# Row maxima over whole rows of 4096 columns in two chunks, with the first conversions and maxima of those chunks placed around the first steps

## The reference, cut to what matters

```python
scores = (Wh @ a1)[:, None] + (We @ a2)[None, :]
e = jnp.where(scores > 0, scores, ALPHA * scores)      # 0.2 in layer 0, 0.01 in layer 1
e = jnp.where(adj > 0, e, NEG_BIG)
attention = jax.nn.softmax(e, axis=1)
h_prime = attention @ entity_embs                      # layer 0; attention @ wh in layer 1
x = _layernorm(x + elu(h_prime + x))                   # layer 0; layer 1: x + out + bias
```

## Time and profile before

| | us |
|---|---|
| median of three runs | 627.31 |
| lowest and highest | 624.94, 627.68 |
| the profiled execution | 624.54 |
| its span in the profile | 622.7 |
| DVE busy | 557.7 |
| ACT busy | 543.5 |
| PE busy | 500.9 |
| POOL busy | 165.6 |

### The profile page before, as it was taken

How to read it: one execution, slowest core, us unless ns; L and a number is a source line. 1 busy time by engine, 2 the same in 40 slices (tenths; PEclk the granted TensorE clock), 3 DMA queues, 4 the chain that set the end, 5 groups by cost and what they waited for, 6 DMA issues and landing times.

```text
span 622.7 us, 14317 instructions
## 1 busy us (share of the span) xinstructions
PE 500.9 (80%) x6039; PEld 232.6 (37%) x6039; DVE 557.7 (90%) x787; ACT 543.5 (87%) x629; POOL 165.6 (27%) x105
## 2 busy tenths in 40 slices
PE   1318777989989799999988877688888888989994
PEld 1214444433444233433444443343333333333352
DVE  5999999899899998989989879779998998889795
ACT  1979998899999997899989989998897999778884
POOL 1171000365027640277001001004410523024041
PEclk9999888999999999999999999998999999999998
DMA  8998996865667735540100000000010001000001
GB/s 183 423 392 322 340 327 214 292 221 188 236 205 272 272 134 238 196 168 2 35 19 2 4 35 1 34 2 2 1 43 1 1 1 35 2 1 1 18 3 26
DMA packets 21340, 76.16 MB, mean 122 GB/s; under 512 B 10412, under 2 KB 11612, under 8 KB 13084
## 3 DMA queue, kind: packets, MB, share of 16 engines
q1 hardware_dynamic: 20472, 74.89, 34.3%
q0 software_dynamic: 112, 0.28, 0.2%
q10 hardware_dynamic: 692, 0.08, 0.1%
HBM read 74.16 MB, written 1.09 MB: 121 GB/s over the span
## 4 chain that ended last, share of the span: by engine, by line
DVE 38%; issue 25%; ACT 16%; PE 15%; DMA 4%; POOL 2%; POOLq 0%; ACTq 0%; DVEq 0%
DVE junk L961 18%; ACT Pm L829 11%; DVE zps L1145 9%; PE acc L1264 8%; PE zps L1326 4%; DMA adj_in<-in_adj 4%; DVE v L938 3%; ACT zps L821 2%; PE acc L1271 1%; ACT v L687 1%; DVE D L981 1%; POOL rstd L633 1%; DVE tot L1030 1%; PE zps L1234 1%; DVE tot L1025 1%
## 5 line engine op out<-in xcount | busy, mean ns | idle before, releaser
L829 ACT ACTIVATE Pm<-zps,ebias 128x1024 f32<-128x1024 f32 (+1 forms) x320 | 292.2, 934 | 34.6 <-DVE zps L1145 29.2
L821 ACT ACTIVATE zps<-S_row,ntau_col 128x1024 f32<-128x1024 f32 (+1 forms) x213 | 202.5, 956 | 5.4
L1326 PE MATMUL zps<-D,v 128*128 128x128 bf16 x2048 | 165.4, 223 | 43.1 <-ACT zps L821 25.8
L1326 PEld LDWEIGHTS zps<-D,v 128*128 128x128 fp8e4 x2048 | 118.3, 99 | 184.5 <-ACT zps L821 87.8
L1264 PE MATMUL acc<-Pm,VE 128*32 128x512 f32 (+2 forms) x1280 | 145.8, 528 | 19.8 <-ACT Pm L829 14.1
L1264 PE MATMUL acc<-Pm,X 128*32 128x512 f32 (+2 forms) x1280 | 138.6, 520 | 23.7 <-ACT Pm L829 22.3
L961 DVE CUSTOM_DVE_ANT_0 junk<-v,adj_in 128x2048 int8<-128x2048 int8 (+3 forms) x88 | 155.8, 1806 | 0.0
L961 DVE CUSTOM_DVE_ANT_0 junk<-v,u_row 128x2048 int8<-128x2048 int8 x64 | 155.3, 2441 | 0.2
L1145 DVE SCALAR_TENSOR_TENSOR zps<-S_row,tau_col,zps 128x1024 f32<-128x1024 f32 (+1 forms) x107 | 110.0, 1051 | 36.7 <-PE zps L1326 35.9
L1271 PE MATMUL acc<-Pm,ones 128*32 128x256 f32 (+1 forms) x1280 | 86.7, 343 | 0.0
L1271 PEld LDWEIGHTS acc<-Pm,ones 128*32 128x32 f32 x1280 | 42.4, 113 | 70.6 <-issue 60.5
(11 more groups left out here) (177 smaller groups left out, 248.4 us busy)
## 6 DMA issues: line engine op xcount, KB each, us to landing
adj_in<-in_adj SPq DMA_DIRECT2D x62, 1024.0 KB, 6.9
S_row<-S_rows_scratch SPq DMA_DIRECT2D x6, 512.0 KB, 3.9
Pm<-in_adj SPq DMA_DIRECT2D x2, 1024.0 KB, 9.8
VE<-in_L_gnn_entity_embs SPq DMA_DIRECT2D x2, 512.0 KB, 5.7
S_row<-S_rows_scratch SPq DMA_DIRECT2D x3, 256.0 KB, 3.2
out<-tAB SPq DMA_DIRECT2D x3, 256.0 KB, 2.6
adj_in<-u_row_scratch SPq DMA_DIRECT2D x2, 256.0 KB, 3.1
S_row<-S_rows_scratch POOLq DMA_DIRECT2D x1, 256.0 KB, 7.1
```

Of the source, the lines that this page charges most:

```text
L821: a.activation(mask_of(n), S_row[:, C % 2, 0:R(C) * P], ACT.Relu, bias=ntau_col[:, layer(C), n % JT:n % JT + 1]).then_inc(seed_done, 1)
L829: a.activation(Pm_of(k, 0, R(C) * P), mask_of(k), ACT.Exp, bias=ebias[:, layer(C), int(seeded(k)), J:J + 1])\
L1326: last = t.matmul(mask[:, r * P:(r + 1) * P], v[:, chunks[C][1] + r, J * P:(J + 1) * P], D[:, C % 2, PART * second + r, :], start=(r * P % ...
```

## The change

For chunks 2 and 3 (`layer(C) == 0 and not narrow(C) and C > 1`) a row's maximum is taken in one piece of 4096 columns instead of two of 2048. `junk` is as large as before; a whole row fills it, so such a piece waits until all pieces before it are done.

The eight pieces of a chunk stand at J = 3, 6, 9, 13, 16, 19, 23 and 26. The sixteen stood at J = 1, 2, 4, 6, 8, 10, 11, 13, 15, 17, 19, 20, 22, 24, 26 and 28. In chunk 3's loop, the eight pieces for chunk 4 (still 2048 wide) stand two steps later than before: 3, 5, 8, 10, 13, 15, 18 and 20.

In chunk 2's loop half 41 (ACT) moves from J = 1 to J = 2, and half 42 (DVE) from J = 3 to J = 0. SP loads in that order: 40, 42, 41. In the loops of chunks 2 and 3 DVE's conversions of J = 0 stand ahead of z0 instead of behind it.

```diff
-        junk = sb("junk", [P, 2, QW], I8)
+        junk = sb("junk", [P, 2 * QW], I8)
...
+            elif layer(C) == 0 and not narrow(C) and C > 1:
+                ends = [0, N]
             else:
                 ends = [0, QW, N]
...
             first, end = max(AHEAD, 2 * chunks[C + 1][1]), 2 * (chunks[C + 1][1] + R(C + 1))
-            return [h for h in range(first, end) if (h - first) * halves_within(C) // (end - first) == J]
+            steps = [i * halves_within(C) // (end - first) for i in range(end - first)]
+            if C == 2:
+
+                steps[1:3] = 2, 0
+            return [first + i for i, step in enumerate(steps) if step == J]
...
-                return [(nxt, i // 2, i % 2) for i in range(n) if i * halves_within(C) // n + 1 == J] + \
+                return [(nxt, i // 2, i % 2) for i in range(n) if i * halves_within(C) // n + MAXIMA_FROM == J] + \
...
-            n = 2 * R(nxt)
-            first = MAXIMA_FROM if layer(C) else 1
-            return [(nxt, i // 2, i % 2) for i in range(n) if first + i * (JT - 2 - first) // n == J]
+            pieces = [(nxt, r, q) for r in range(R(nxt)) for q in range(len(segments(nxt)))]
+            n = len(pieces)
+
+            first, end = (MAXIMA_FROM, JT - 2) if layer(C) or n == R(nxt) else (1, JT - 2)
+            return [pieces[i] for i in range(n) if first + i * (end - first) // n == J]
...
-                    wait_v(dve, 2 * rt + q)
+                    wait_v(dve, 2 * rt + (cols.stop - 1) // HALF)
...
-                if at >= 2:
-                    dve.wait_ge(max_done, at - 1)
-                d.tensor_tensor_reduce(out=junk[:, at % 2, 0:cols.stop - cols.start],
+                width = cols.stop - cols.start
+                whole = width > QW
+                done = at if whole or junk_whole[0] else at - 1
+                junk_whole[0] = whole
+                if done > 0:
+                    dve.wait_ge(max_done, done)
+                first = 0 if whole else at % 2 * QW
+                d.tensor_tensor_reduce(out=junk[:, first:first + width],
...
+                    by_vector = [H for H in halves_at(C, J) if H // 2 not in ACT_TILES]
+                    if C > 1 and J == 0:
+                        for H in by_vector:
+                            compare(H)
                     if not seeded(k):
...
-                    for H in halves_at(C, J):
-                        if H // 2 not in ACT_TILES:
+                    if C <= 1 or J:
+                        for H in by_vector:
                             compare(H)
```

More of the change, by code:

```diff
@@ L939, in compare @@
                                 ALU.is_gt, ALU.subtract, saturate=False).then_inc(compared, 1)
-            maxima = [0]
+            maxima, junk_whole = [0], [False]
             def row_max(C, r, q):
```

## The result

| | before | after |
|---|---|---|
| median, us (six runs each, side by side) | 626.95 | 633.75 |
| lowest and highest | 624.94, 627.85 | 630.25, 637.89 |
| the profiled execution | 624.54 | 630.25 |
| its span | 622.7 | 628.4 |
| DVE busy | 557.7 | 550.2 |

The ratio of after to before is 1.0121, with a 95% interval from 1.0088 to 1.0155: 7.6 us slower (5.5 to 9.7). The forecast was +6.0 us and 633.3 us.

What follows compares the result with a forecast made beforehand. The prediction took DVE and ACT together, neither leading alone, to bound the kernel. Its terms, +2.0 (chunk 1) + 4.8 (chunk 2) - 0.8 (chunk 3) = +6.0 us, gave 633.3 us on the median of 627.31; range 627.5 to 637.5.

Steps and rivals of the forecast that it cites:

- What bounds the kernel: Chunks 1 and 2: DVE and ACT both nearly always busy, neither leading alone; z27 is where DVE's backlog reaches ACT.
- The price of a whole row: DVE's maxima: 4096 columns cost 4.34 us against 4.42 for two halves, saving 0.08 us a tile, 0.6 us per chunk.
- POOL and DVE take turns: Each waits for the other's current instruction; a POOL instruction just behind a whole row's start waits 4.34 instead of 2.2 us.
- Chunk 1: ACT's 2.00 us at the elu stay, z27 comes 3.2 us later, PE absorbs 1.2; chunk 2 starts 2.0 us later.
- Chunk 2: From z5 to z27: more row work, 4.0 us wait at the elu, new DVE idle time; z27 4.8 us later.
- Chunk 3: z2 no longer behind a maximum, ACT's 1.85 us wait goes, but the copy waits for PE's projection: 0.8 us gained.
- much slower: Rival: PE idle 3 us and more before z27, twice, and its clock falls, or PE absorbs nothing; 637.6 or above; chance 0.08.
- That POOL gets its turn ahead of the row: Rival, both chunks: POOL's L576 goes before the whole row, the elu does not wait; +1.7, 629.0 us; chance 0.20.
- The faster rival: POOL's work slides wholly into DVE's waits; chunk 2's z27 comes at 234.5; -4.8 us, 622.5; chance 0.10.
- The sum: Whole kernel: +2.0 (chunk 1) + 4.8 (chunk 2) - 0.8 (chunk 3) = +6.0 us; bounds +1.9 to +10.3.

Runs made afterwards that it cites:

- e1: The changed kernel with each whole row as two halves again, both at the whole row's step; first steps stay changed: 631.2 us, ratio 1.0083 to before.
- e5: The changed kernel with the last whole row of chunks 1 and 2's loops at J = 28 and chunk 2's reciprocal at J = 6: 626.5 us, ratio 1.0001.
- e6: The changed kernel with only the reciprocal of chunk 2's loop one step earlier, at J = 6: 631.66 us, ratio 1.0085 to before.
- e2: The kernel before with only the changed first steps and chunk 3's later maxima; all maxima halves at their old steps: 625.28 us, ratio 0.9976.
- e4: The changed kernel with the last whole row in the loops of chunks 1 and 2 at J = 28, behind z27, instead of J = 26: 630.08 us, ratio 1.0060.
- e3: Whole rows at the steps of the changed kernel, with the first steps of the kernel before: 634.8 us, ratio 1.0137 to before.
- e7: The changed kernel with the whole row of tile 24 in chunk 2's loop at J = 18 instead of 16: 632.39 us, ratio 1.0107 to before.
- e8: e2 with the half row of J = 26 at J = 28 in chunks 1 and 2's loops, and chunk 1's reciprocal at J = 8: 623.25 us, ratio 0.9949.
- e10: e5 with the reciprocal of chunk 1's loop one step earlier too, at J = 8: 625.35 us, ratio 0.9987 to before.

## Why the prediction was right, point by point

**What bounds the kernel.** Right: neither DVE nor ACT leads alone. DVE lost 7.5 us of work and the kernel 5.7 us of time.

**The price of a whole row.** Right. The group of all whole rows (busy time, mean ns of one, idle time ahead and what ended it):

```profile
L975 DVE CUSTOM_DVE_ANT_0 junk<-v,u_row 128x4096 int8<-128x4096 int8 x16 | 71.9, 4492 | 5.1 <-ACT v L695 5.0
```

One undisturbed lasts 4.42 us, and from the last row at 238.02 to z27 at 242.37 are 4.35 us, against 4.34 forecast and 2 x 2.21 for two halves. A merged pair saves 0.07, not the 0.156 us that the prediction worked out by the Trainium skill ("VectorE: DVE Perf Modes", section on the TRN2 errata). The page's 150 cycles are the fixed part in the duration of one instruction, and the traces agree with that: at 0.96 GHz and one column a cycle, 2048 and 4096 columns would last 2.29 and 4.42 us by such an estimate, and they do. What a merged pair saves is less, because neighbours overlap by 0.07 us. The 5.0 us of idle time in this row are the waits for tiles 20 and 24, which the sum had missed.

**POOL and DVE take turns.** Right, and the step from which the most followed. For chunk 2's elu 4.0 us were forecast and 4.00 measured; in chunk 1 2.0 and 1.98. For the idle time ahead of the first sum of chunk 2 2.2 us were forecast and 2.33 measured, ahead of the scores 1.1 and 1.08. The Trainium skill ("SBUF — State Buffer", section on the two separate sides) has the rule: a DVE operation in a two-port mode or with two SBUF inputs, and a GpSimd operation that reads SBUF, share a pair of ports, and the one that starts first holds it for its whole instruction. L589's 5.33 us, which end 1.1 us behind the whole row, agree. e1 with its halves (1.96 us instead of 4.00) and e5 and e6 (none, where the reciprocal comes earlier) show that the row's length and its place make that wait.

**Chunk 1.** Right in kind, a little too large. z7 came 2.4 us earlier than before (112.11 against 114.55). 1.1 us of that were there at the chunk's first masks (96.50 against 97.59), ahead of every changed step. The rest goes with PE's granted clock between 97 and 115 us, 1.00 against 0.91, and not with the rows: e2, which has half rows at their old steps, ran at 1.00 there as well and has the same 15.6 us from the first masks to z7 as the kernel after, where the execution of before has 17.0; e1 and e4, whose rows are moved, ran at 0.91 and have 17.2 and 17.1. Counted from z7, z27 is 2.4 us later (3.2 forecast), ACT waits 3.13 us for it (3.8), and z0 of chunk 2 is 1.5 us later (2.0).

**Chunk 2.** The mechanism was right, the size too small: counted from z0, z27 is 6.5 us later, not 4.8, and ACT waits 3.91 us for it, not 2. Two terms were off, in opposite directions. DVE's busy time between z5 and z27 is the third number with a bracket, 52.91 us before and 53.30 after:

```profile
183.78:236.83 53.05, 46.52 (x554) 19.78 (x546) 52.91 (x48) 52.37 (x51) 29.29 (x11) 1.00 0.61 213
```

```profile
182.43:242.37 59.94, 50.34 (x578) 21.26 (x576) 53.30 (x36) 52.72 (x51) 29.86 (x12) 0.97 0.57 199
```

DVE's idle time there grew from next to nothing to 6.6 us, where 3.3 were forecast. The term that was missing is DVE's wait for ACT. A whole row needs both halves of its tile, and for tiles 20 and 24 the second half is ACT's work. For tile 24 it is late by ACT's own stall at the elu: counted from z0, that conversion starts 3.8 us later than before, and DVE waits 2.98 us; in e5 and e6, where the elu does not stall, DVE does not wait for it. The prediction counted the elu's stall for ACT, but not that DVE then waits for what ACT converts behind it. The 1.99 us for tile 20 have another cause, as they stand 20 us ahead of the elu: the change itself moved ACT's conversion of half 41 to J = 2, one step ahead of the row, and e3, with the old first steps, does not have this wait. It cost nothing, as z5 has 1.90 us of idle time ahead of it all the same.

DVE's own work between z5 and z27 grew by 0.4 us, where 3.9 - 2.3 + 0.2 = 1.8 us were forecast. The instructions that POOL lengthens lose 9.4 us together in the kernel before and 5.4 in the kernel after, so 4.0 us came back and not 2.3: whole rows are fewer and longer, and POOL takes fewer turns against a busy DVE. Without this second error the forecast of chunk 2 would have been short by 3.1 us, not by 1.7.

**Chunk 3.** z0 came 6.38 us later. Besides z27, 0.84 us lie between the two, where PE's product took 1.93 instead of 1.06 us after 2.99 us of idle time and the granted clock was 0.89. That is the mechanism of the rival "much slower", in one of the two places where that looked for it (at z27 of chunk 1 PE stood idle for 1.17 us only), and it cost 0.84 us, not several: from that product to the next of its form there are 3.35 us instead of 2.19, and a part came back, as PE then ran at 1.98 us a step. The experiments bear it out: from z27 of chunk 2 to z0 of chunk 3 there are 9.9 us in the kernel after, 10.9 in e6, where PE stood idle for 4.67 us, and 8.9 in e7, where it stood idle for 0.75 us and no product was slow. From z0 of chunk 3 to chunk 4 the kernel gains about 0.6 us (0.8 forecast): the first masks of chunk 4 come 5.8 us later than before. The way was the one forecast: ACT's 1.85 us for z2 are gone, and at the copy it waits 0.93 us for PE's projection instead:

```profile
259.59 0.66 ACT L779 ACTIVATE o<-zps 128x256 f32<-128x256 f32 x2 [0.93 <-PE zps L1262]
```

**The rivals.** That POOL gets its turn ahead of the row fell with the waits of 1.98 and 4.00 us at the elu. The faster rival fell with z27 of chunk 2, which came later and not earlier: between 170 and 243 us DVE was busy 11 us less, but only because it waited for PE, POOL and ACT.

**The sum.** Put right by these readings it is 6.0 - 0.5 (chunk 1) + 1.7 (chunk 2) + 0.8 (the clock) + 0.2 (chunk 3) = 8.2 us. The profiled executions differ by 5.7, and by 8.1 if the 2.4 us at the start are taken out, which are not the change's. The ratio gives 7.6 (5.5 to 9.7). So by the traces the forecast of 6.0 was some 2 us short (by the two medians alone the difference is 6.8 us, and the interval of the ratio takes in the 6.0).

That the profiled execution came out at 630.25 us, where 630.5 stood in the prediction, is luck, and so are the first masks of chunks 3 and 4 at 251.6 and 321.3 us (251.9 and 321.5 forecast): 2.4 us that were won ahead of z7, by no step of the change, hide the 2.2 us that the forecast was short.

**What stays open.** How much of the loss falls to the length alone is only bounded: e1 and after differ by 0.4% with intervals that overlap, e8 and e10 by 0.4% with ones that don't, but with other steps as well. In chunk 1, z27 came 0.8 us less late than forecast, and no run takes that apart.

## What to carry to other kernels

Before merging or moving pieces, find the last place on the engine at which it waits for somebody, and count what stands between it and the next instruction that another engine awaits: here one whole row there cost ACT 3 us twice, and moving it and one small reciprocal took the whole loss back (e5). A long instruction on DVE is a long turn that POOL must wait out, so put whatever POOL waits for in front of short instructions, not of long ones. And a stall that is given to another engine comes back: whoever needs that engine's next products waits as well.

## What the runs showed of the hardware

- POOL's multiplication of 128x512 lasts 1.18 us alone, 3.22 beside half rows and 5.33 beside a whole row. It does not take longer in proportion to its own work, but ends about 1.1 us after the DVE instruction that it has met.
- A short idle time of PE can be enough for its granted clock to fall, and its length alone does not decide. In the kernel after, the clock is 0.89 in the 15 us around each of three idle times in the loops of chunks 1 and 2, and 1.00 in the stretches between them (130 to 155 and 215 to 235 us): 1.68 us behind the elu of chunk 1, 4.53 us at the elu of chunk 2, and 2.99 us ahead of the product that needs the exponential of z27. Behind each PE ran 3 to 3.5 us at the lower level and then as before. In the kernel before, 1.69 us of idle time at the first of these places was followed by no slow product. PE's timeline there, the mask product and the product behind it, first before, then after:

```profile
125.55 0.62 PE L1326 MATMUL zps<-D,v 128*128 128x128 bf16 x8 [1.69 <-ACT zps L821]
126.58 1.06 PE L1264 MATMUL acc<-Pm,VE 128*32 128x512 f32 x8 [0.41 <-ACT Pm L829]
```

```profile
123.09 0.62 PE L1345 MATMUL zps<-D,v 128*128 128x128 bf16 x8 [1.68 <-ACT zps L829]
124.12 1.24 PE L1283 MATMUL acc<-Pm,VE 128*32 128x512 f32 x8 [0.41 <-ACT Pm L837]
```

And at the elu of chunk 2 in the kernel after, two products of the same form, and the mask product ahead of the first:

```profile
200.23 1.03 PE L1345 MATMUL zps<-D,v 128*128 128x128 bf16 x8 [4.53 <-ACT zps L829]
201.26 1.94 PE L1283 MATMUL acc<-Pm,VE 128*32 128x512 f32 x8
...
204.27 1.07 PE L1283 MATMUL acc<-Pm,VE 128*32 128x512 f32 x8
```

- A wait of DVE for a transfer of 2.4 us ahead of the conversion of half 42 (at 167.55 us) cost nothing: PE's mask product for z0 ended at 168.82 us, and z0 started at 168.86.
